# A windowed attention block with its MLP and divisive normalisation, in fp32: the first normalised set is copied by VectorE instead of ScalarE, the MLP's way down is split around the transposes, and odd halves take their fourth strip from the other end

## The chip, the cores and the metric

The kernel runs on one core of a Trainium2 chip. The metric is the device time of one execution in microseconds, the median over several executions. A core has five engines that run their own instruction streams and wait for each other by semaphores: TensorE (PE in the profile, with PEld for its weight loads), VectorE (DVE), ScalarE (ACT), GpSimd (POOL) and SyncE (SP), which here issues the DMAs. TensorE reads SBUF and writes PSUM; PSUM has eight banks, all of them in use.

## What is computed

The input is (4, 96, 128, 128) in fp32: four images of 96 channels. The block does layer normalisation over the channels, attention with 6 heads of 16 in shifted windows of 8x8 tokens, a projection and a residual, a second layer normalisation, an MLP of 96 to 384 to 96 with an exact GELU and a second residual, and at last a generalised divisive normalisation over the channels. Cut to what matters:

```python
y = _ln(x, norm1_w, norm1_b)
y = jnp.roll(y, (-ss, -ss), axis=(1, 2))
y = y.reshape(B, H // ws, ws, W // ws, ws, C).transpose(0, 1, 3, 2, 4, 5).reshape(-1, N, C)
qkv = y @ qkv_w.T + qkv_b
...
attn = jnp.einsum('bhnd,bhmd->bhnm', q, k) + mask
attn = jax.nn.softmax(attn, axis=-1)
out = jnp.einsum('bhnm,bhmd->bnhd', attn, v).reshape(-1, N, C) @ proj_w.T + proj_b
...
x = shortcut + out
h1 = jax.nn.gelu(_ln(x, norm2_w, norm2_b) @ mlp_w1.T + mlp_b1, approximate=False)
x = x + (h1 @ mlp_w2.T + mlp_b2)
...
denom_sq = jnp.einsum('nchw,ic->nihw', x * x, gamma_eff) + beta_eff
return x * jax.lax.rsqrt(denom_sq)
```

The mask is not zero only for windows in the last row and in the last column of windows of an image.

## The kernel before

The image is cut into 64 units of 8 rows (16 windows of 64 tokens), and a unit into two halves of 8 windows (512 tokens). There are 128 halves, numbered A; an even half holds windows 0 to 7 of its unit and an odd half windows 8 to 15. The kernel is a software pipeline, written out by hand: in round H each engine runs its list of stages (a function `steps` for each engine), each stage on the half H + offset. The offsets are TURN_IN 4 (transposes of the input to tokens by channels, and statistics), TURN_OUT 3 (normalised tokens transposed back), QK 1, ATTEND 0, PROJECT -2, MLP -3, UP -4 (up to 384), SETTLE -5 (down to 96), DIVIDE -6. So a round holds one stage each of several halves, and the time is about 128 rounds. Order between engines comes from semaphores alone.

The stages that matter here, in the order in which a round takes them:

- TensorE: `scores` (k and q of six windows per strip; windows' masks are added by one more small matmul each, line 1045), `project_k` and `project_q`, `times_v` (line 1061), `denominators`, `sum_probs`, `project`, `mlp_down` (lines 1108 and 1111), `turn_run` (transposes of the probabilities, line 936, mixed with those of both normalised sets, line 942), `project_v` (line 1007), `mlp_up` 0 and 1 (line 1096), `turn_in` of the input and of the second residual stream (lines 923 and 928), `mlp_up` 2.
- VectorE: row maxima and subtraction of the scores (`max_scores`, `shift_scores`, lines 792 and 799, first for the fourth strip in `pv_bank`, then for three banks), `normalise` twice, `first_residual` (815), `divide` (808), `second_residual` (824), `outputs` (830), `split_y2` (770: the low part of the second normalised set), `v_blocks` (783, four copies), `statistics` (721, eight), `variances` (734 to 743).
- ScalarE: copies of k and q (556, 550), four exponentials (564), logarithms and inverses, an activation table load (514), `y2_copy` (544: the high part of the second normalised set), `y1_copy` (538: the first normalised set, two instructions of 96x256, out of PSUM into window order), copies of the transposed probabilities (575), three GELUs (593), a table load.

The channels of a half lie in strips: with 96 channels in groups of 32, three groups fill partitions 0 to 95, and partitions 96 to 127 hold a fourth strip, which takes a fourth part of the half's tokens. In the attention, `in_strips` puts three pairs of windows (MAIN, 384 tokens) in the three groups and the pair LAST in the fourth strip; `divide` writes `attended`, and `move_attended` carries the fourth strip by three DMAs to its place.

Two waits tie the first normalised set to other stages. `split_y2` has `dve.wait_ge(y_ready[0], ...)` beside its own `y_ready[1]`, and `turn_in` waits for `y_ready[0]` and `y2_split`, since it writes to the banks (`turn_banks`) that hold both sets. `y_ready[0]` is raised by `y1_copy`, `y_ready[1]` by `y2_copy`. The banks of `mlp_up` are handed on in a fixed order (`MM_ITEMS`): `mlp_up` 0 waits for `x2_ready` (`first_residual`), `mlp_up` 1 for `x3_ready` (`second_residual`), `mlp_up` 2 for the first GELU.

Of the kernel before, what the change touches and what calls it, by code (L numbers as in the profile page):

```python
# [23 lines left out]
HEADS, WIN, SHIFT = 6, 8, 4  # L24
# [43 lines left out]
def window_block(nc, x, qmask, kmask, ident, head_mask, ones_pair, norm1_w, norm1_b, qkv_t, qkv_b,  # L68
# [8 lines left out]
    with ctx:  # L77
# [229 lines left out]

        SOFTMAX_ORDER = (GROUPS, 0, 1, 2)
# [14 lines left out]
        def _(sp):  # L323
# [46 lines left out]
            def move_attended(A):  # L370

                wait_alone(sp, attended_ready, A + 1)
                for j in range(HEAD_PAIRS):
                    sp.dma_start(attended[group(j), MAIN:HALF], attended[strip, group(j, 128)])\
                        .then_inc(attended_moved, 16)
# [127 lines left out]
        def _(act):  # L503
# [27 lines left out]
            def y1_copy(A):  # L531
                act.wait_ge(y_turned[0], 2 * (A + 1))
                by_window = y1[0:DIM, unit_slot(A, Y_SLOTS), :]\
                    .rearrange("c (n q x) -> c n q x", q=WIN, x=WIN)[:, :, chunks_of(A)[0]:chunks_of(A)[-1] + 1, :]
                for r in range(2):
                    dst = by_window[:, r * HALF_WINDOWS:(r + 1) * HALF_WINDOWS, :, :]
                    src = normed_columns(0)[:, :, r, :].rearrange("c q (n x) -> c n q x", x=WIN)
                    made = nc.scalar.activation(dst, src, ACT.Copy)  # L538
                made.then_inc(y_ready[0], 1)

# [18 lines left out]
            def softmax_exp(A, g):  # L559
# [3 lines left out]
                dst = probs[:, :, LAST, :, :] if g == GROUPS else probs[:, g, 0:LAST, :, :]  # L563
# [45 lines left out]
            def steps(run, H):  # L609
# [15 lines left out]
                run(y1_copy, TURN_OUT)  # L625
# [11 lines left out]
        def _(dve):  # L637
# [126 lines left out]
            def split_y2(A):  # L764

                dve.wait_ge(y_ready[1], A + 1)
                dve.wait_ge(y_ready[0], min(A - MLP + TURN_OUT + 1, HALVES))
                lo, hi = (half_of(tile[0:DIM, :], A).rearrange("c (q r t) -> c q r t", r=2, t=64)
                          for tile in (y2_lo, y2_hi))
                nc.vector.tensor_tensor(lo, normed_columns(1), hi, ALU.subtract).then_inc(y2_split, 1)  # L770

# [32 lines left out]
            def divide(A):  # L804
# [3 lines left out]
                nc.vector.tensor_tensor(attended[:, 0:MAIN], pv_bank[:, 0:MAIN], inv_sum[:, :],  # L808
# [25 lines left out]
            def steps(run, H):  # L834
# [31 lines left out]
        def _(pe):  # L866
# [118 lines left out]

            def project_k(A):
# [6 lines left out]
                in_strips(mm_bank("k", A), wk, y1_windows(A, 0, 2 * LAST), y1_windows(A, 2 * LAST))\  # L993
                    .then_inc(k_made, 1)

            def project_q(A):
# [3 lines left out]
                in_strips(mm_bank("q", A), wq, y1_windows(A, 0, 2 * LAST), y1_windows(A, 2 * LAST))\  # L1000
# [49 lines left out]
            def times_v(A):  # L1050
# [5 lines left out]
                for turn in range(2 * LAST):  # L1056
                    at, n = turn // 2, turn % 2
                    first = turn * TOKENS
                    for s in range(STRIPS):
                        m, p = (s, at) if s < HEAD_PAIRS else (at, LAST)  # L1060
# [6 lines left out]
            def sum_probs(A):  # L1067
# [3 lines left out]
                for m in range(HEAD_PAIRS):  # L1071
                    nc.tensor.matmul(sum_bank[group(m), 0:MAIN], ones_pair_sb[:, :],
                                     probs_t[:, A % 2, m, 0:LAST, :], start=True, stop=True)
                for m in range(HEAD_PAIRS):
                    made = nc.tensor.matmul(sum_bank[strip, group(m, 128)], ones_pair_sb[:, :],  # L1075
                                            probs_t[:, A % 2, m, LAST, :], start=True, stop=True)
# [23 lines left out]
            def mlp_down(A):  # L1100

                pe.wait_ge(gelu_ready, HID_CHUNKS * (A + 1))
                mm_wait("mlp2", A)
                to = mm_bank("mlp2", A)
                for n in range(HID_CHUNKS):
# [7 lines left out]
                made.then_inc(mlp2_made, 1)  # L1113
# [6 lines left out]
            def steps(run, H):  # L1120
# [20 lines left out]
                run(turn_in, PROJECT, 1)  # L1141
                run(mlp_up, UP, 2)
# [54 lines left out]
```

## Time and profile before

| | |
|---|---|
| median of 3 runs | 1757.68 us (1756.24 to 1758.75) |
| profiled execution, its own time | 1756.11 us |
| span of the profiled execution | 1754.3 us |
| mean granted TensorE clock | 0.991 |
| busy: PE, PEld, DVE, ACT, POOL | 95%, 83%, 81%, 85%, 21% |

The span is the time from the first to the last instruction of the core; the execution's own time is 1.8 us more. A busy share is an average over the whole span, and PE's counts matmuls whose ends are modelled.

### The profile page before, as it was taken

What the parts mean: (1) busy time and instruction counts of PE and PEld (TensorE: products, weight loads), DVE (VectorE), ACT (ScalarE), POOL (GpSimd) and SP (SyncE); (2) the same over time, 40 slices, a digit from 0 to 9 for tenths busy, and PEclk for the clock granted to TensorE, in tenths of its full rate; (3) what the DMA queues carried; (4) which work ended last, traced back from release to release, by engine and by line L of the source; (5) the groups of instructions that cost most, each with busy time, mean ns of one, the idle gap of its engine ahead of it and who ended that gap; (6) DMA issues with size and microseconds to landing.
All of it is one profiled execution on the core that took longest, in us unless ns stands there. A gap on an engine that the chain in (4) does not pass through costs nothing.

```text
span 1754.3 us, 83088 instructions
## 1 busy us (share of the span) xinstructions
PE 1662.1 (95%) x33524; PEld 1464.1 (83%) x33524; DVE 1423.0 (81%) x4142; ACT 1487.8 (85%) x2957; POOL 361.1 (21%) x459
## 2 busy tenths in 40 slices
PE   5899999999999999999999999999999999999995
PEld 3688888888888888888888888888888888888874
DVE  5788888888888888888888888888888888888871
ACT  2688888888888888888888888888888888888884
POOL 2121221221221221221221221221222222222111
PEclk9999999999999999999999999999999999999997
DMA  2112122122122122122122122122121222222111
GB/s 57 47 51 64 55 61 62 54 64 59 55 61 62 54 61 62 54 67 57 54 69 56 53 68 57 53 68 57 55 66 56 56 66 57 57 64 57 46 34 32
DMA packets 179169, 100.38 MB, mean 57 GB/s; under 512 B 26868, under 2 KB 178790, under 8 KB 178790
## 3 DMA queue, kind: packets, MB, share of 16 engines
q1 hardware_dynamic: 178228, 94.96, 19.5%
q8 instruction: 269, 4.41, 1.1%
q14 instruction: 110, 0.90, 0.2%
q10 hardware_dynamic: 562, 0.11, 0.0%
HBM read 32.05 MB, written 25.17 MB: 33 GB/s over the span
## 4 chain that ended last, share of the span: by engine, by line
PE 71%; DVE 17%; issue 5%; ACT 5%; DMA 1%; SPq 0%; POOL 0%; DVEq 0%; POOLq 0%
PE mm_bank L906 10%; PE mm_bank L1111 10%; PE mm_bank L1096 8%; PE score_banks L936 7%; PE pv_bank L1061 6%; PE mm_bank L904 6%; DVE stats L721 5%; PE mm_bank L1108 5%; PE pv_bank L1007 4%; DVE v_block L783 4%; PE turn_banks L942 4%; PE score_banks L1075 3%; PE score_banks L1037 3%; DVE row_max L792 2%; DVE shifted L799 2%
## 5 line engine op out<-in xcount | busy, mean ns | idle before, releaser
L514 ACT ACT_TABLE_LOAD x256 | 328.4, 1283 | 4.6
L564 ACT ACTIVATE probs<-shifted 128x384 f32<-128x384 f32 x512 | 265.7, 519 | 32.0 <-DVE shifted L799 29.0
L1108 PE MATMUL mm_bank<-hidden,w 128*32 128x384 f32 x2304 | 277.4, 492 | 0.1
L1111 PE MATMUL mm_bank<-hidden,w 128*32 128x128 f32 x2304 | 276.8, 275 | 0.0
L593 ACT ACTIVATE hidden<-mm_bank 128x512 f32<-128x512 f32 x384 | 238.4, 621 | 42.2 <-PE mm_bank L1096 41.5
L1111 PEld LDWEIGHTS mm_bank<-hidden,w 128*32 128x32 f32 x2304 | 254.4, 111 | 1.2
L469 POOL TENSOR_TENSOR x<-x,b_bias 128x384 f32<-128x384 f32 x128 | 105.7, 826 | 716.7 <-PE turn_banks L928 716.7
L770 DVE TENSOR_TENSOR y_lo<-turn_banks,y_hi 96x512 fp32r<-96x512 f32 x128 | 87.9, 687 | 197.2 <-ACT y L538 194.3
L575 ACT ACTIVATE probs_t<-score_banks 128x512 f32<-128x512 f32 x384 | 220.1, 617 | 0.0
L792 DVE TENSOR_REDUCE row_max<-score_banks 128x6 f32<-128x384 f32 x384 | 199.4, 547 | 0.0
L799 DVE TENSOR_TENSOR shifted<-score_banks,row_max 128x384 f32<-128x384 f32 x384 | 199.3, 546 | 0.0
L721 DVE BATCH_NORM_STATS2 stats<-turn_banks 128x6 f32<-128x96 f32 x1024 | 181.7, 249 | 17.1 <-PE turn_banks L923 11.2
L783 DVE COPY v_block<-pv_bank 64x192 f32<-64x192 f32 x512 | 180.4, 352 | 11.7 <-PE pv_bank L1007 6.5
L936 PE MATMUL score_banks<-ident_sb,probs 64*128 64x64 f32 x3072 | 181.8, 229 | 4.0 <-ACT probs L564 2.3
L1096 PE MATMUL mm_bank<-y_hi,w_hi 97*128 97x512 f32 x384 | 172.9, 450 | 0.1
L936 PEld LDWEIGHTS score_banks<-ident_sb,probs 64*128 64x128 f32 x3072 | 146.5, 138 | 30.0 <-issue 24.4
L1061 PEld LDWEIGHTS pv_bank<-probs_t,v_block 128*32 128x32 f32 x6144 | 97.2, 110 | 74.6 <-issue 74.1
L1061 PE MATMUL pv_bank<-probs_t,v_block 128*32 128x64 f32 x6144 | 114.3, 221 | 44.4 <-DVE shifted L799 40.5
L1096 PE MATMUL mm_bank<-y_lo,w_hi 97*128 97x512 f32 x384 | 152.0, 396 | 0.0
L1096 PE MATMUL mm_bank<-y_hi,w_lo 97*128 97x512 f32 x384 | 150.6, 392 | 0.0
L1037 PE MATMUL pv_bank<-k_block,q 32*64 32x128 f32 x1536 | 147.5, 284 | 0.0
L1007 PE MATMUL pv_bank<-wv,y 97*128 97x96 f32 x1024 | 145.8, 286 | 0.0
(110 smaller groups left out, 4568.1 us busy)
## 6 DMA issues: line engine op xcount, KB each, us to landing
x_ext<-in_x SPq DMA_DIRECT2D x128, 192.0 KB, 3.2
k_block<-k SPq DMA_DIRECT2D x256, 96.0 KB, 2.0
out<-o_ext SPq DMA_DIRECT2D x64, 192.0 KB, 2.8
x_ext<-in_x SPq DMA_DIRECT2D x128, 48.0 KB, 2.8
attended<-attended SPq DMA_DIRECT2D x384, 16.0 KB, 1.8
x<-x SPq DMA_DIRECT2D x384, 16.0 KB, 1.8
out<-o_ext SPq DMA_DIRECT2D x64, 96.0 KB, 2.6
out<-o_ext SPq DMA_DIRECT2D x128, 48.0 KB, 2.1
```

Source lines behind the costliest of these rows:

```text
L514: nc.scalar.preload_act_table_set(name)
L564: nc.scalar.activation(dst, shifted[:, g, :, :].rearrange("t (i e) k -> t i e k", e=TILE_HEADS), ACT.Exp).then_inc(probs_ready, 1)
L593: nc.scalar.activation(hidden[:, n, :], mm_bank(f"mlp1_{n}", A)[:, :], ACT.Gelu)\
L721: made = nc.vector.bn_stats(stats[:, (H + 1) % 2, ln, n, :], chunk)
L783: made = nc.vector.tensor_copy(to, values[:, :, :, e, :])
L792: nc.vector.tensor_reduce(row_max[:, g, :], group_scores(g), op=ALU.max, axis=AX.X)\
L799: nc.vector.tensor_tensor(shifted[:, g, :, :], group_scores(g), row_max[:, g, :].unsqueeze(2) .broadcast_to([128, LAST * TILE_HEADS, TOKENS]),
L936: return nc.tensor.transpose(score_banks[:, bank, first:first + TOKENS], probs[half, m, p, :, :], ident_sb[half, half])
L1061: made = nc.tensor.matmul(pv_bank[group(s), first:first + TOKENS], v_block[:, (A % 2) * HALF_WINDOWS + 2 * p + n, m, :], probs_t[:, A % 2, ...
L1096: made = nc.tensor.matmul(mm_bank(f"mlp1_{n}", A)[:, :], w[:, cols], tokens, start=part == 0, stop=part == 2)
L1108: nc.tensor.matmul(to[group(j), 0:MAIN], w2[:, n, group(j)], hidden[:, n, 128:HALF], start=first, stop=last)
L1111: made = nc.tensor.matmul(to[strip, group(n, 128)], w2[:, c, group(n)], hidden[:, c, 0:128], start=c == 0, stop=c == HID_CHUNKS - 1)
```

## The change

It has three parts.

1. `y1_copy` goes from ScalarE to VectorE, as two copies of 96x256 that come behind `split_y2` and ahead of `v_blocks`. `split_y2` no longer waits for `y_ready[0]`. On VectorE, `outputs` now comes ahead of `second_residual`.
2. `mlp_down` gets the list of its steps: steps 0 and 1 are done ahead of `turn_run` and step 2 behind it. `mlp_up` 1 goes behind both `turn_in`.
3. In odd halves the main pairs of windows are 1 to 3 and the fourth strip takes pair 0, where it took pair 3. In even halves nothing changes. The same number of instructions works on the same sizes; window 15, the only masked one of most odd halves, now lies in the main strips.

```diff
+        def main_pairs(A):
+            return range(A % 2, A % 2 + LAST)
+        def side_pair(A):
+            return 0 if A % 2 else LAST
+        def main_tokens(A):
+            return slice(A % 2 * 128, A % 2 * 128 + MAIN)
+        def side_tokens(A):
+            return slice(side_pair(A) * 128, side_pair(A) * 128 + 128)
...
                 for j in range(HEAD_PAIRS):
-                    sp.dma_start(attended[group(j), MAIN:HALF], attended[strip, group(j, 128)])\
+                    first = main_tokens(A).start + 128 * j
+                    sp.dma_start(attended[group(j), side_tokens(A)], attended[strip, first:first + 128])\
                         .then_inc(attended_moved, 16)
...
-            def y1_copy(A):
-                act.wait_ge(y_turned[0], 2 * (A + 1))
...
-                    made = nc.scalar.activation(dst, src, ACT.Copy)
-                made.then_inc(y_ready[0], 1)
...
                 run(y2_copy, MLP)
-                run(y1_copy, TURN_OUT)
                 run(probs_t_copy, ATTEND, 0)
...
             def split_y2(A):
                 dve.wait_ge(y_ready[1], A + 1)
-                dve.wait_ge(y_ready[0], min(A - MLP + TURN_OUT + 1, HALVES))
...
+            def y1_copy(A):
+                dve.wait_ge(y_turned[0], 2 * (A + 1))
...
+                for r in range(2):
+                    dst = by_window[:, r * HALF_WINDOWS:(r + 1) * HALF_WINDOWS, :, :]
+                    src = normed_columns(0)[:, :, r, :].rearrange("c q (n x) -> c n q x", x=WIN)
+                    made = nc.vector.tensor_copy(dst, src)
+                made.then_inc(y_ready[0], 1)
...
                 run(divide, ATTEND - 1)
+                run(outputs, DIVIDE)
                 run(second_residual, SETTLE)
-                run(outputs, DIVIDE)
                 run(split_y2, MLP)
+                run(y1_copy, TURN_OUT)
                 run(v_blocks, ATTEND)
...
             def window_of(A, r, i, n):
-                return (A % 2) * HALF_WINDOWS + 2 * (LAST if r == GROUPS else i) + n
+                return (A % 2) * HALF_WINDOWS + 2 * (side_pair(A) if r == GROUPS else main_pairs(A)[i]) + n
...
-            def mlp_down(A):
-                pe.wait_ge(gelu_ready, HID_CHUNKS * (A + 1))
-                mm_wait("mlp2", A)
+            def mlp_down(A, steps):
+                if steps[0] == 0:
+                    pe.wait_ge(gelu_ready, HID_CHUNKS * (A + 1))
+                    mm_wait("mlp2", A)
...
-                for n in range(HID_CHUNKS):
+                for n in steps:
...
-                made.then_inc(mlp2_made, 1)
+                if steps[-1] == HID_CHUNKS - 1:
+                    made.then_inc(mlp2_made, 1)
...
-                run(mlp_down, SETTLE)
+                run(mlp_down, SETTLE, range(0, 2))
                 turn_run(H)
+                run(mlp_down, SETTLE, range(2, HID_CHUNKS))
                 run(project_v, ATTEND)
                 run(mlp_up, UP, 0)
-                run(mlp_up, UP, 1)
                 run(turn_in, TURN_IN, 0)
...
                 run(turn_in, PROJECT, 1)
+                run(mlp_up, UP, 1)
                 run(mlp_up, UP, 2)
```

The first place is VectorE in the middle of a round, from `first_residual` on. The row of before, with the semaphores that each instruction waits for (`y_ready1` is `y1_copy`'s, `y_ready2` is `y2_copy`'s):

```order
L815 TENSOR_TENSOR x<-mm_bank,x_ext 128x384 [waits x3_ready,x_biased,proj_made]
L808 TENSOR_TENSOR attended<-pv_bank,inv_sum 128x384 [waits proj_made,pv_made,inv_sum_ready]
L824 TENSOR_TENSOR x<-mm_bank,x 128x384 [waits out_ready,sq_ready,x2_biased,mlp2_made]
L830 TENSOR_TENSOR o_ext<-x,inv_den 128x6x64 [waits out_stored1,inv_den_ready]
L770 TENSOR_TENSOR y_lo<-turn_banks,y_hi 96x512 [waits y_ready1,y_ready2]
L783 COPY v_block<-pv_bank 64x4x3x16 [waits v_made]
L783 COPY v_block<-pv_bank 64x4x3x16 x3
```

And the same place with the change:

```order
L831 TENSOR_TENSOR x<-mm_bank,x_ext 128x384 [waits x3_ready,x_biased,proj_made]
L824 TENSOR_TENSOR attended<-pv_bank,inv_sum 128x384 [waits proj_made,pv_made,inv_sum_ready]
L846 TENSOR_TENSOR o_ext<-x,inv_den 128x6x64 [waits out_stored1,inv_den_ready]
L840 TENSOR_TENSOR x<-mm_bank,x 128x384 [waits out_ready,sq_ready,x2_biased,mlp2_made]
L776 TENSOR_TENSOR y_lo<-turn_banks,y_hi 96x512 [waits y_ready2]
L785 COPY y<-turn_banks 96x8x32 [waits y_turned1]
L785 COPY y<-turn_banks 96x8x32
L799 COPY v_block<-pv_bank 64x4x3x16 [waits v_made]
L799 COPY v_block<-pv_bank 64x4x3x16 x3
```

`second_residual` now stands directly ahead of `split_y2`, and the two copies of the first normalised set stand between `split_y2` and the four copies of v.

The second place is TensorE from the last transpose of `turn_run` to the end of `mlp_up`. Before:

```order
L936 MATMUL score_banks<-ident_sb,probs 128x64
L1007 MATMUL pv_bank<-wv,y1 128x96 x4
L1096 MATMUL mm_bank0<-y2_hi,w1_hi 128x512
L1096 MATMUL mm_bank0<-y2_hi,w1_lo 128x512
L1096 MATMUL mm_bank0<-y2_lo,w1_hi 128x512
L1096 MATMUL mm_bank1<-y2_hi,w1_hi 128x512
L1096 MATMUL mm_bank1<-y2_hi,w1_lo 128x512
L1096 MATMUL mm_bank1<-y2_lo,w1_hi 128x512
L923 MATMUL turn_banks<-ident_sb,x_ext 128x96 x4
L928 MATMUL turn_banks<-ident_sb,x2 128x128 x3
```

With the change:

```order
L953 MATMUL score_banks<-ident_sb,probs 128x64
L1131 MATMUL mm_bank1<-hidden,w2 32x384 x3
L1134 MATMUL mm_bank1<-hidden,w2 32x128 x3
L1029 MATMUL pv_bank<-wv,y1 128x96 x4
L1118 MATMUL mm_bank0<-y2_hi,w1_hi 128x512
L1118 MATMUL mm_bank0<-y2_hi,w1_lo 128x512
L1118 MATMUL mm_bank0<-y2_lo,w1_hi 128x512
L940 MATMUL turn_banks<-ident_sb,x_ext 128x96 x4
L945 MATMUL turn_banks<-ident_sb,x2 128x128 x3
L1118 MATMUL mm_bank1<-y2_hi,w1_hi 128x512
```

The last step of the way down now follows the transposes, and only one of the two `mlp_up` groups is left between `project_v` and `turn_in`.

The third place is TensorE in `scores` of an odd half with one masked window. Before:

```order
L1037 MATMUL score_banks<-k_block,q 64x128 x6
L1037 MATMUL pv_bank<-k_block,q 64x128 x2
L1045 MATMUL pv_bank<-k_masks,q_quadrants 64x128
L1037 MATMUL score_banks<-k_block,q 64x128 x6
L1037 MATMUL pv_bank<-k_block,q 64x128 x2
L1045 MATMUL pv_bank<-k_masks,q_quadrants 64x128
L1037 MATMUL score_banks<-k_block,q 64x128 x6
L1037 MATMUL pv_bank<-k_block,q 64x128 x2
L1045 MATMUL pv_bank<-k_masks,q_quadrants 64x128
L904 MATMUL mm_bank1<-y1,wk 32x384 x3
```

With the change:

```order
L1059 MATMUL score_banks<-k_block,q 64x128 x6
L1059 MATMUL pv_bank<-k_block,q 64x128 x2
L1059 MATMUL score_banks<-k_block,q 64x128 x6
L1059 MATMUL pv_bank<-k_block,q 64x128 x2
L1059 MATMUL score_banks<-k_block,q 64x128 x6
L1059 MATMUL pv_bank<-k_block,q 64x128 x2
L1067 MATMUL score_banks<-k_masks,q_quadrants 64x128 x3
L921 MATMUL mm_bank1<-y1,wk 32x384 x3
```

The three mask matmuls went from one group of partitions, one behind each set of scores, to three different groups of partitions, all behind the last set.

## Rows read from the trace of the kernel before

**Rows 1.** The page: busy time, share and instructions of each engine.

```profile
PE 1662.1 (95%) x33524; PEld 1464.1 (83%) x33524; DVE 1423.0 (81%) x4142; ACT 1487.8 (85%) x2957; POOL 361.1 (21%) x459
```

**Rows 2.** Waits from 100 to 1700 us: total, times, longest.

```profile
DVE y_lo L770 <- ACT y L538: 189.0, 119, 1.6
...
PE pv_bank L1061 <- DVE shifted L799: 39.9, 60, 1.3
```

**Rows 3.** Timeline of VectorE, 806 to 812 us: start, length, what.

```profile
806.20 0.69 DVE L770 TENSOR_TENSOR y_lo<-turn_banks,y_hi 96x512 fp32r<-96x512 f32 x1 [1.58 <-ACT y L538]
806.80 1.45 DVE L783 COPY v_block<-pv_bank 64x192 f32<-64x192 f32 x4
808.28 1.42 DVE L721 BATCH_NORM_STATS2 stats<-turn_banks 128x6 f32<-128x96 f32 x8
...
811.12 0.56 DVE L799 TENSOR_TENSOR shifted<-pv_bank,row_max 128x384 f32<-128x384 f32 x1
```

**Rows 4.** Timeline of TensorE, 811 to 821 us.

```profile
811.83 0.88 PE L1061 MATMUL pv_bank<-probs_t,v_block 128*32 128x64 f32 x48 [0.67 <-DVE shifted L799]
...
814.45 0.52 PE L1108 MATMUL mm_bank<-hidden,w 128*32 128x384 f32 x3
...
816.06 0.52 PE L1108 MATMUL mm_bank<-hidden,w 128*32 128x384 f32 x3
...
816.58 0.77 PE L936 MATMUL score_banks<-ident_sb,probs 64*128 64x64 f32 x17
...
817.83 0.22 PE L936 MATMUL score_banks<-ident_sb,probs 64*128 64x64 f32 x1
817.99 1.13 PE L1007 MATMUL pv_bank<-wv,y 97*128 97x96 f32 x8
818.90 0.47 PE L1096 MATMUL mm_bank<-y_hi,w_hi 97*128 97x512 f32 x1
...
820.36 0.49 PE L923 MATMUL turn_banks<-ident_sb,x_ext 96*128 96x96 f32 x4
```

**Rows 5.** Timeline of VectorE, 815 to 820 us.

```profile
815.07 0.45 DVE L760 TENSOR_TENSOR y_tok<-turn_banks,rstd 128x288 f32<-128x288 f32 x1
815.44 0.55 DVE L815 TENSOR_TENSOR x<-mm_bank,x_ext 128x384 f32<-128x384 f32 x1
...
816.68 0.56 DVE L824 TENSOR_TENSOR x<-mm_bank,x 128x384 f32<-128x384 f32 x1 [0.23 <-PE mm_bank L1111]
817.16 0.55 DVE L830 TENSOR_TENSOR o_ext<-x,inv_den 128x384 f32<-128x384 f32 x1
...
819.30 0.69 DVE L770 TENSOR_TENSOR y_lo<-turn_banks,y_hi 96x512 fp32r<-96x512 f32 x1 [1.59 <-ACT y L538]
```

**Rows 6.** Timeline of ScalarE, 816 to 819 us.

```profile
816.19 1.28 ACT L514 ACT_TABLE_LOAD   x1
818.06 0.59 ACT L544 ACTIVATE y_hi<-turn_banks 96x512 fp32r<-96x512 f32 x1 [0.58 <-PE turn_banks L942]
```

**Rows 7.** Timeline of TensorE: scores, k, q and the next product with v.

```profile
808.72 0.35 PE L1037 MATMUL score_banks<-k_block,q 32*64 32x128 f32 x6
...
809.63 0.52 PE L904 MATMUL mm_bank<-y,wk 97*32 97x384 f32 x3
...
821.82 0.35 PE L1037 MATMUL score_banks<-k_block,q 32*64 32x128 f32 x6
...
823.32 0.52 PE L904 MATMUL mm_bank<-y,wk 97*32 97x384 f32 x3
...
824.31 0.50 PE L904 MATMUL mm_bank<-y,wq 97*32 97x384 f32 x3
...
824.91 0.88 PE L1061 MATMUL pv_bank<-probs_t,v_block 128*32 128x64 f32 x48
```

**Rows 8.** Groups of VectorE instructions by shape: count, busy us, mean ns, idle before.

```profile
L783 DVE COPY v_block<-pv_bank 64x192 f32<-64x192 f32 x512 | 180.4, 352 | 11.7 <-PE pv_bank L1007 6.5
...
L701 DVE CAST w_hi<-w 97x384 fp32r<-97x384 f32 x1 | 0.4, 352 | 0.0
```

More of the change, by code:

```diff
@@ L529, in rstd_pair @@
                     .then_inc(rstd_ready, 1)
-            def y1_copy(A):
-                act.wait_ge(y_turned[0], 2 * (A + 1))
[L533 to L537, printed above, removed]
-                    made = nc.scalar.activation(dst, src, ACT.Copy)
-                made.then_inc(y_ready[0], 1)
             def y2_copy(A):
@@ L562, in softmax_exp @@
                     wait(act, probs_turned[bank], A)
-                dst = probs[:, :, LAST, :, :] if g == GROUPS else probs[:, g, 0:LAST, :, :]
+                pairs = slice(main_pairs(A)[0], main_pairs(A)[-1] + 1)
+                dst = probs[:, :, side_pair(A), :, :] if g == GROUPS else probs[:, g, pairs, :, :]
                 nc.scalar.activation(dst, shifted[:, g, :, :].rearrange("t (i e) k -> t i e k", e=TILE_HEADS),
@@ L770, in split_y2 @@
                 nc.vector.tensor_tensor(lo, normed_columns(1), hi, ALU.subtract).then_inc(y2_split, 1)
+            def y1_copy(A):
+                dve.wait_ge(y_turned[0], 2 * (A + 1))
+                by_window = y1[0:DIM, unit_slot(A, Y_SLOTS), :]\
+                    .rearrange("c (n q x) -> c n q x", q=WIN, x=WIN)[:, :, chunks_of(A)[0]:chunks_of(A)[-1] + 1, :]
+                for r in range(2):
[3 more added lines that the diff above has]
+                made.then_inc(y_ready[0], 1)
             def v_blocks(A):
@@ L807, in divide @@
                 wait(dve, proj_made, A)
-                nc.vector.tensor_tensor(attended[:, 0:MAIN], pv_bank[:, 0:MAIN], inv_sum[:, :],
+                nc.vector.tensor_tensor(attended[:, main_tokens(A)], pv_bank[:, 0:MAIN], inv_sum[:, :],
                                         ALU.mult).then_inc(attended_ready, 1)
@@ L984, in turn_run, with qk_windows @@
                             made.then_inc(probs_turned[2], 1)
+            def qk_windows(A):
+                side = 2 * side_pair(A)
+                return y1_windows(A, 2 * main_pairs(A)[0], 2 * main_pairs(A)[-1] + 2), y1_windows(A, side, side + 2)
             def project_k(A):
@@ L992, in project_k @@
                 mm_wait("k", A)
-                in_strips(mm_bank("k", A), wk, y1_windows(A, 0, 2 * LAST), y1_windows(A, 2 * LAST))\
+                in_strips(mm_bank("k", A), wk, *qk_windows(A))\
                     .then_inc(k_made, 1)
@@ L999, in project_q @@
                 mm_wait("q", A)
-                in_strips(mm_bank("q", A), wq, y1_windows(A, 0, 2 * LAST), y1_windows(A, 2 * LAST))\
+                in_strips(mm_bank("q", A), wq, *qk_windows(A))\
                     .then_inc(q_made, 1)
@@ L1059, in times_v @@
                     for s in range(STRIPS):
-                        m, p = (s, at) if s < HEAD_PAIRS else (at, LAST)
+                        m, p = (s, main_pairs(A)[at]) if s < HEAD_PAIRS else (at, side_pair(A))
                         made = nc.tensor.matmul(pv_bank[group(s), first:first + TOKENS],
@@ L1072, in sum_probs @@
                     nc.tensor.matmul(sum_bank[group(m), 0:MAIN], ones_pair_sb[:, :],
-                                     probs_t[:, A % 2, m, 0:LAST, :], start=True, stop=True)
+                                     probs_t[:, A % 2, m, main_pairs(A)[0]:main_pairs(A)[-1] + 1, :], start=True, stop=True)
                 for m in range(HEAD_PAIRS):
                     made = nc.tensor.matmul(sum_bank[strip, group(m, 128)], ones_pair_sb[:, :],
-                                            probs_t[:, A % 2, m, LAST, :], start=True, stop=True)
+                                            probs_t[:, A % 2, m, side_pair(A), :], start=True, stop=True)
                 made.then_inc(sums_made, 1)
```

## The prediction

> **What bounds the kernel now.** The page alone points at TensorE: 95% busy, ScalarE 85%, VectorE 81% [rows 1]. But ends of matmuls are modelled, so I read the waits next. Two matter [rows 2]: VectorE's `split_y2` waits for ScalarE's `y1_copy` in 119 rounds, 1.6 us each, and TensorE's product with v (line 1061) waits for the subtraction of the fourth strip's maxima (799) in 60 rounds, 0.67 us each. So TensorE does wait, in every other round. Then the timeline. I count from the start of `times_v` in one round, 811.83 = 0, and write places as such offsets.
>
> VectorE's side [rows 3]: once `split_y2` starts, it works without a stop: the four copies of v start 0.60 later, statistics and variances follow, the strip's subtraction ends at 811.68, and `times_v` starts at 811.83. From `split_y2` to `times_v` are 5.63, from the copies of v to it 5.03. TensorE's side [rows 4]: from `times_v` to the way down 2.62, the way down in six blocks of (816.06 - 814.45) / 5 = 0.32, the transposes at 4.75, the next work behind them (`project_v`) at 6.16. Then ScalarE: y2 at 6.23 [rows 6], y1 behind it, and `split_y2` at 819.30 - 811.83 = 7.47 [rows 5]. 7.47 + 5.61 = 13.08 (it ends at 824.91 [rows 7]), the round; from one `split_y2` to the next it is 13.10 [rows 3, 5]. This loop goes through all three engines: TensorE to the last transpose, ScalarE for two copies, VectorE to the subtraction. It holds in odd rounds too. There TensorE's scores take 823.32 - 821.82 = 1.50 where the even round's take 0.91 [rows 7], because of the masked window. But q's last block starts at 824.31, TensorE would be free at 824.63, and `times_v` starts at 824.91, when VectorE is done. TensorE has about 0.3 to spare in odd rounds and 0.85 in even ones. So the 0.59 for the masks is hidden today.
>
> **The change, part by part.**
>
> *Way down split.* Four of six blocks stay ahead of the transposes: they start 2 x 0.32 = 0.65 earlier, at 4.10, and end, with the 1.41 from 816.58 to 817.99 [rows 4], at 5.51. What they need is there: `normalise` ends at 815.07 + 0.45 = 815.52 [rows 5], offset 3.69, and ScalarE's last exponential stands two instructions of the same size ahead of the table load at 816.19 [rows 6], so it ends near 815.3. ScalarE's table load ends at 816.19 + 1.28 = 817.47, offset 5.64 [rows 6]; y2's copy then runs 5.64 to 6.23, and `split_y2` could start at 6.34, with the 0.11 from copy to VectorE. That is 1.1 earlier than today.
>
> *But `second_residual` is late now.* It waits for the whole way down. The two blocks behind the transposes start at 5.51 and 5.83; today VectorE starts 816.68 - 816.06 = 0.62 behind the last block's start [rows 4, 5], so 6.45. It stands ahead of `split_y2` and holds it for 0.48, the distance to the next instruction (816.68 to 817.16 [rows 5]). So `split_y2` starts at 6.93, not 6.34: it gains 0.54, where the waits of [rows 2] seemed to promise 1.6. `outputs` ahead of it costs nothing; it falls into VectorE's idle time between 4.5 and 6.45.
>
> *Two copies on VectorE.* They lie on the chain. No row shows a 96x256 copy on VectorE. A 128x384 instruction takes 0.55 and a 128x288 one 0.45, 1.04 ns an element; 256 elements give 0.42 busy [rows 5]. What counts is the distance from start to start: 0.60 for 512 elements [rows 3], 0.37 for 288 (815.07 to 815.44 [rows 5]), so 0.34 for 256. Two are 0.68. The other bound is the copies of v: four of 192 elements take (808.28 - 806.80) / 4 = 0.37 each, more than their busy 0.352 [rows 3, 8]; with 64 elements more (0.067) that is 0.43, two are 0.86. I take 0.68, since the copies of v alternate between partitions 0 and 64, and y1's all stand at partition 0, as the instructions of [rows 5] do.
>
> The Trainium skill (VectorE: DVE Perf Modes, section "Two Vector instructions with no wait between them") says it as a rule: an instruction waits for all earlier ones when its start quadrant differs from that of the last access, else it may start into the tail of the one before. By this rule the trace agrees: 0.37 against 0.352 busy for v, 0.46 to 0.48 against 0.55 for the rest. By the rule the pair costs 0.68, without it 0.86.
>
> *Sum.* v's copies start at 6.93 + 0.60 + 0.68 = 8.21, today at 8.07. The round is 8.21 + 5.03 = 13.24 against 13.10: 0.14 longer. Over 128 rounds that is 18 us. Fill and drain lack some stages, and I leave them as they are.
>
> *TensorE's path, to see that it doesn't bind.* `turn_in` waits for y1's second copy: 6.93 + 0.60 + 0.34 + 0.42 = 8.29, plus 0.15 from VectorE to TensorE (811.68 to 811.83 [rows 3, 4]) is 8.44. Today `turn_in` starts at 8.53 [rows 4] and scores follow 1.46 later [rows 4, 7]. Now a second `mlp_up` lies between, which I take at 0.70 (two fill 818.90 to 820.36, 0.73 each with the first one's start-up [rows 4]): scores at 10.60. Even rounds: 0.91 for them, 1.33 for k and q, `times_v` possible at 12.84, below 13.24. Odd rounds with today's masks: 13.43, above it. So the fourth strip's move matters: its three masks go to three groups of partitions, where tiles work beside each other: the even round's 0.91 holds three sets of eight tiles, 0.04 a tile, so three masks cost some 0.11: 12.95. It saves TensorE 0.48 in 64 rounds and the kernel nothing against today, because VectorE ends last. TensorE idles near 0.65 ahead of `turn_in`; today's stall of 0.67 [rows 4] in every other round goes with a mean granted clock of 0.991, so I cost no fall to 1.2 GHz.
>
> *The others.* ScalarE loses two copies, and its GELU for `mlp_up` 2 comes some 0.6 later, with the table load and the copies of k and q behind it; in today's odd rounds all of that comes 0.59 later too, behind the longer scores [rows 7], and the loop doesn't notice. x3's three DMAs on SP's queue start 1.6 later (`second_residual` at 6.45, today 4.85), behind them those of `attended`; `square` and the product that read x3 come much later, behind `turn_in`'s `bias_x2` on POOL. I cost both at nothing; were x3 late, `denominators` at 0.66 of the next round would wait, one for one.
>
> **Rivals.**
>
> *Copies at full distance.* 0.86 instead of 0.68 puts 0.17 more into each round: 13.41, or 0.31 x 128 = 40 us, 1797. For it: v's copies, the only PSUM copies in the trace. Against: their alternating partitions.
>
> *The masks stay in line.* If they cost 0.59 in main strips too, TensorE binds odd rounds at 13.43: 0.19 x 64 = 12 us more, 1788. It decides from 0.4 us upward. Against it: they lie on three groups of partitions, as the tiles of a set do.
>
> *No pause behind the transposes.* TensorE pauses between shapes: 0.20 before the transposes and 0.16 behind them (817.83 to 817.99 [rows 4]). If the way down's second part starts without the 0.16, VectorE gains it: 0.14 - 0.16, no change, 1756. Against: the shapes still change there. The split also adds one such change, ahead of `project_v`, 0.16 to 0.20 by these rows; it falls into the 0.65 ahead of `turn_in` and costs nothing (without that cover, 0.16 x 128 = 20 us). The Trainium skill (TensorEngine Tiling (Array Packing), "Key Properties") says that changing the tiling mode drains TensorE. By this rule, with which the two pauses agree, the 0.16 stays and my sum holds; without the rule the round would be today's.
>
> *Faster: copies at double rate.* Line 701 converts 384 elements in 352 ns [rows 8], where 384 take 0.55 [rows 5], so a one-source instruction can run at two elements a cycle. Then 256 elements cost 0.20 from start to start, two 0.40: 0.14 - 0.28 = -0.14, 18 us less, 1740. It decides below 0.27 a copy. Against: line 701 reads SBUF; v's copies read PSUM, as y1's do, and their 352 ns for 192 elements is the slow rate.
>
> **How the numbers follow.** The sum 0.14 x 128 = 18 us is made against the profiled execution's 1756.11 us, 1.6 below the median, so 1774 there and 1776 as a median. Chances: my sum 0.5; full distance 0.13; masks in line or another path of TensorE 0.12; no change 0.13; double rate, or a gain that I don't see, 0.12. All but the last two are slower: 0.75. A measurement of this kernel tells about 0.2% (3.5 us) from nothing. The range 1754 to 1798 leaves out only the faster cases and holds the others; if only slower ones are counted, it is 1766 to 1798.
>
> **What would show it.** Between `split_y2` starts 13.2 to 13.3 us in odd and even rounds; `split_y2` waiting for `second_residual` and not for ScalarE; y1's copies 0.42 busy and 0.34 apart; an idle TensorE of 0.5 to 0.8 ahead of line 940 in nearly every round, and one of 0.3 ahead of line 1083 that waits for line 815; masks behind the scores in about 0.1. I am wrong if the round is under 13.1, which needs a shorter distance from the transposes to v's copies than 2.70, or if TensorE arrives last in `times_v`.

## The result and the profile after

The change makes the kernel 1.1% slower. Its median is 1777.85 us (1773.97 to 1778.8, 4 runs), against 1756.96 us (1756.02 to 1758.75, 4 runs) for the kernel before: a ratio of 1.0113, 95% interval 1.0098 to 1.0127. The forecast was 1776.

The profiled execution took 1773.97 us, with a span of 1772.2 and a granted clock of 0.993. The page, where [rows 1] had 95, 83, 81, 85 and 21%:

```profile
span 1772.2 us, 82960 instructions
PE 1676.4 (95%) x33524; PEld 1422.3 (80%) x33524; DVE 1494.0 (84%) x4398; ACT 1436.4 (81%) x2701; POOL 366.1 (21%) x459
```

VectorE's busy time has grown by 71 us and ScalarE's has shrunk by 51. Then the waits of the same stretch as [rows 2], 100 to 1700 us: engine, line and what it waited for, us in total, times, longest.

```profile
ACT hidden L601 <- PE mm_bank L1118: 196.7, 240, 1.3
DVE x L840 <- PE mm_bank L1134: 166.5, 121, 1.7
PEld turn_banks L940 <- issue: 73.9, 118, 0.6
...
POOL x_sq L493 <- DMA x<-x: 36.3, 33, 2.0
...
PE pv_bank L1083 <- DVE shifted L815: 15.4, 53, 1.0
```

`split_y2`'s wait of 1.6 us for ScalarE is gone. In its place, in 121 rounds, VectorE waits 1.4 for the end of the way down, in `second_residual` (840). The timeline shows the piece of VectorE that answers to [rows 3, 5]: start, duration, instruction, and the idle time ahead of it in brackets.

```profile
824.17 0.56 DVE L840 TENSOR_TENSOR x<-mm_bank,x 128x384 f32<-128x384 f32 x1 [1.46 <-PE mm_bank L1134]
824.65 0.68 DVE L776 TENSOR_TENSOR y_lo<-turn_banks,y_hi 96x512 fp32r<-96x512 f32 x1
825.25 0.74 DVE L785 COPY y<-turn_banks 96x256 f32<-96x256 f32 x2
825.91 1.45 DVE L799 COPY v_block<-pv_bank 64x192 f32<-64x192 f32 x4
827.39 1.42 DVE L728 BATCH_NORM_STATS2 stats<-turn_banks 128x6 f32<-128x96 f32 x8
828.91 0.29 DVE L741 TENSOR_TENSOR mean_gap<-stats 128x8 f32<-128x8 f32 x1
829.12 0.16 DVE L743 TENSOR_TENSOR within<-stats 128x8 f32<-128x8 f32 x1
```

And TensorE, for [rows 4]. `times_v` (1083) of this round had started at 817.63.

```profile
823.22 0.52 PE L1131 MATMUL mm_bank<-hidden,w 128*32 128x384 f32 x3
...
823.57 0.50 PE L1131 MATMUL mm_bank<-hidden,w 128*32 128x384 f32 x3
...
824.01 1.13 PE L1029 MATMUL pv_bank<-wv,y 97*128 97x96 f32 x8
...
826.09 0.52 PE L940 MATMUL turn_banks<-ident_sb,x_ext 96*128 96x96 f32 x4 [0.23 <-issue]
...
828.99 0.45 PE L1067 MATMUL score_banks<-k_masks,q_quadrants 4*64 4x128 f32 x6
...
830.89 0.49 PE L1083 MATMUL pv_bank<-probs_t,v_block 128*32 128x64 f32 x21
```

The second part of the way down starts at 823.22 - 817.63 = 5.59 behind `times_v`, and `second_residual` at 6.54. This round is 0.1 late in all of it: the medians over 110 rounds are 5.49 and 6.45, where 5.51 and 6.45 had been worked out. Places given from here on as one number are such medians, counted from the start of `times_v`.

From one `times_v` to the next I took the distance over 110 rounds of each timeline, from the tenth on. The median was 13.088 and is 13.175; 99 of the 110 rounds lay within 0.02 of it, and now 59 do. The mean was 13.106 and is 13.225: 0.119 x 128 = 15 of the 18 us between the two spans. Of these, 0.087 x 128 = 11 us are in the regular round, and 4 come from single longer rounds: 7 of 110 were over 13.2, up to 13.6, and 25 are, up to 14.15. The rest is in the first and last rounds. So the total is as forecast, but the forecast had 0.14 in every round.

One instruction leads further. `mean_gap` is a subtraction of 128x8 elements, and VectorE's other instructions of its size take 0.16 or 0.17. It took 0.29 here, and in other rounds 0.17, or up to 0.7 (once 0.99). In the same trace, this is where it is alone:

```profile
1371.79 0.17 DVE L741 TENSOR_TENSOR mean_gap<-stats 128x8 f32<-128x8 f32 x1
```

And this is a slow round, GpSimd's `square` (line 493) and VectorE's `mean_gap`:

```profile
1596.09 1.04 POOL L493 TENSOR_TENSOR x_sq<-x 96x512 f32<-96x512 f32 x1 [0.49 <-DMA x<-x]
...
1596.57 0.59 DVE L741 TENSOR_TENSOR mean_gap<-stats 128x8 f32<-128x8 f32 x1
```

`square` ends at 1596.09 + 1.04 = 1597.13 and `mean_gap` at 1596.57 + 0.59 = 1597.16: they end together. In the round above `mean_gap` ends at 829.20, and `square`:

```profile
828.13 1.03 POOL L493 TENSOR_TENSOR x_sq<-x 96x512 f32<-96x512 f32 x1 [0.19 <-issue]
```

It ends at 829.16. In the whole stretch `mean_gap` takes over 0.2 in 101 of 121 rounds, and in all 101 it ends 0.02 to 0.03 behind a `square`. The 119 `mean_gap` of 128x8 took 332 ns each before, and take 296 with the change. So the kernel before already paid some 0.15 here, in nearly every round, inside the 5.03 us that the prediction took over as VectorE's work. Its lines, from the round that ends at 824.91:

```profile
822.15 1.03 POOL L476 TENSOR_TENSOR x_sq<-x 96x512 f32<-96x512 f32 x1
822.90 0.31 DVE L734 TENSOR_TENSOR mean_gap<-stats 128x8 f32<-128x8 f32 x1
```

From `square`'s start to the next `times_v` are 824.91 - 822.15 = 2.76, and with the change 830.89 - 828.13 = 2.76 too. The medians say the same: `square` started at 10.33 and starts at 10.42, and 2.76 later the round is over, at 13.09 and at 13.175. So in both kernels it is `square` that sets the end of the regular round. Before, it started as soon as GpSimd's `bias_x2` was done; now it starts 0.26 behind the landing of x3's DMAs (1.76 before).

### The profile page after: what moved, and what is told of

It reads as the page before. It is cut to its first block, busy times and chain, and to the rows that moved or that the text cites. A ratio compares the mean times of both kernels' runs of the same rounds, so it can differ in the third digit from the quotient of the medians.

```text
span 1772.2 us, 82960 instructions
## 1 busy us (share of the span) xinstructions
PE 1676.4 (95%) x33524; PEld 1422.3 (80%) x33524; DVE 1494.0 (84%) x4398; ACT 1436.4 (81%) x2701; POOL 366.1 (21%) x459
## 4 chain that ended last, share of the span: by engine, by line
PE 73%; DVE 20%; issue 4%; DMA 1%; ACT 1%; SPq 0%; POOL 0%; DVEq 0%; POOLq 0%; ACTq 0%
PE mm_bank L923 10%; PE mm_bank L1134 10%; PE mm_bank L1118 8%; PE score_banks L953 7%; PE pv_bank L1083 6%; PE mm_bank L1131 6%; PE mm_bank L921 6%; DVE stats L728 5%; PE pv_bank L1029 4%; PE turn_banks L959 4%; PE score_banks L1059 3%; DVE v_block L799 3%; PE score_banks L1097 3%; DVE y L785 2%; PE turn_banks L940 2%
## 5 line engine op out<-in xcount | busy, mean ns | idle before, releaser
L601 ACT ACTIVATE hidden<-mm_bank 128x512 f32<-128x512 f32 x384 | 229.3, 597 | 221.7 <-PE mm_bank L1118 209.8
L1131 PE MATMUL mm_bank<-hidden,w 128*32 128x384 f32 x2304 | 302.3, 495 | 0.1
L1134 PE MATMUL mm_bank<-hidden,w 128*32 128x128 f32 x2304 | 300.5, 276 | 0.0
L1134 PEld LDWEIGHTS mm_bank<-hidden,w 128*32 128x32 f32 x2304 | 243.6, 111 | 1.2
L840 DVE TENSOR_TENSOR x<-mm_bank,x 128x384 f32<-128x384 f32 x128 | 71.4, 558 | 178.5 <-PE mm_bank L1134 178.5
L583 ACT ACTIVATE probs_t<-score_banks 128x512 f32<-128x512 f32 x384 | 212.7, 591 | 0.9 <-PE score_banks L953 0.8
L728 DVE BATCH_NORM_STATS2 stats<-turn_banks 128x6 f32<-128x96 f32 x1024 | 182.0, 251 | 12.4 <-PE turn_banks L940 7.0
L493 POOL TENSOR_TENSOR x_sq<-x 96x512 f32<-96x512 f32 x128 | 132.7, 1037 | 78.2 <-DMA x<-x 61.6
L1029 PEld LDWEIGHTS pv_bank<-wv,y 97*128 97x128 f32 x1024 | 124.7, 192 | 24.8 <-issue 24.4
```

The costliest lines, as they stand in the source:

```text
L583: nc.scalar.activation(dst, src, ACT.Copy).then_inc(probs_t_ready, 1)
L601: nc.scalar.activation(hidden[:, n, :], mm_bank(f"mlp1_{n}", A)[:, :], ACT.Gelu)\
L728: made = nc.vector.bn_stats(stats[:, (H + 1) % 2, ln, n, :], chunk)
L1029: made = nc.tensor.matmul(pv_bank[:, p * DIM:(p + 1) * DIM], y1_windows(A, 2 * p, 2 * p + 2), wv[:, :], start=True, stop=True)
L1131: nc.tensor.matmul(to[group(j), 0:MAIN], w2[:, n, group(j)], hidden[:, n, 128:HALF], start=first, stop=last)
L1134: made = nc.tensor.matmul(to[strip, group(n, 128)], w2[:, c, group(n)], hidden[:, c, 0:128], start=c == 0, stop=c == HID_CHUNKS - 1)
```

## The experiments

All times are medians. The kernel before, run again beside them, has 1757.4 us beside e3, e4, e5 and e7, 1757.2 beside e6, e8, e9 and e10, and 1758.2 beside e11 and e12. "Round" is the median distance of `times_v`, in even and in odd rounds where they differ.

| kernel | us | ratio to before, 95% interval | round |
|---|---|---|---|
| before | 1757 | | 13.09 |
| after | 1777.85 | 1.0113 [1.0098, 1.0127] | 13.17 |
| e3_way_whole | 1746.62 | 0.9936 [0.9922, 0.9951] | 12.99 |
| e4_strip_back | 1792.39 | 1.0201 [1.0184, 1.0218] | 13.18 / 13.44 |
| e5_square_late | 1761.56 | 1.0023 [1.0012, 1.0034] | 13.06 |
| e7_copy_back | 1760.71 | 1.0011 [1.0001, 1.0021] | 13.17, 17 of 110 at 12.4 to 12.6 |
| e6_before_square_late | 1741.19 | 0.9900 [0.9876, 0.9924] | 12.94 |
| e8_copy_back_square_late | 1706.74 | 0.9711 [0.9687, 0.9736] | 12.45 / 12.64 |
| e9_strip_back_square_late | 1727.43 | 0.9820 [0.9795, 0.9844] | 12.45 / 13.04 |
| e10_way_whole_square_late | 1741.72 | 0.9903 [0.9882, 0.9924] | 12.94 / 12.97 |
| e11_up_ahead_square_late | 1759.62 | 1.0009 [0.9999, 1.0020] | 13.05 |
| e12_residual_behind_square_late | 1748.32 | 0.9949 [0.9932, 0.9965] | 12.90 |

**e3_way_whole**: the changed kernel with the way down whole again, ahead of the transposes, and `second_residual` ahead of `outputs`.

```diff
+                run(second_residual, SETTLE)
                 run(outputs, DIVIDE)
-                run(second_residual, SETTLE)
...
-                run(mlp_down, SETTLE, range(0, 2))
+                run(mlp_down, SETTLE, range(0, HID_CHUNKS))
                 turn_run(H)
-                run(mlp_down, SETTLE, range(2, HID_CHUNKS))
```

> The changed kernel with the way down whole again, ahead of the transposes, and second_residual ahead of outputs as before; y1's copies stay on VectorE, mlp_up 1 stays behind turn_in. My theory (VectorE's chain ends last): the transposes start at 4.75 after times_v, y2's copy ends near 6.82, split_y2 starts at 6.93, the same as the 6.92 of the changed kernel, so v's copies start at 8.18 again. The split buys nothing. But second_residual comes 1.6 us earlier, x3's DMAs land earlier, and GpSimd's square is over when mean_gap starts: round 13.06 to 13.12, no rounds of 13.4 and more, 1754 to 1762 us. Rival (only the start of split_y2 counts, GpSimd doesn't): as the changed kernel, 1774 to 1779. Rival (TensorE's pauses between shapes and its idle ahead of turn_in set the time): one pause of 0.16 less in each round, and 13.0, 1757.

Measured: 1746.62, below the range and below the kernel before. `split_y2` starts at 6.85, `mean_gap` takes 177 ns on average, and the round is 12.99. With y1 off ScalarE and x3 early, `square` starts at 10.12, and it ends 0.03 behind the start of `mean_gap` (11.12). So the split of the way down, with the order that goes with it on VectorE, costs this kernel 31 us; 16 of them go when `square` is moved (e5).

**e4_strip_back**: the changed kernel with the fourth strip on pair 3 in odd halves too.

```diff
-            return range(A % 2, A % 2 + LAST)
+            return range(0, LAST)
...
-            return 0 if A % 2 else LAST
+            return LAST
...
-            return slice(A % 2 * 128, A % 2 * 128 + MAIN)
+            return slice(0, MAIN)
```

> The changed kernel with the fourth strip taken from pair 3 in odd halves too. My theory: the masks cost 0.59 in odd rounds again instead of 0.11. TensorE reaches times_v at 10.53 + 1.50 + 1.33 = 13.36 or later in odd rounds, where VectorE allows 13.17; even rounds stay. Odd rounds 13.4 to 13.45, 60 of them: 12 to 17 us more than the changed kernel, 1789 to 1794. Rival (the strip's end changes nothing, VectorE ends last in any case): 1777.

Measured: 1792.39, inside the range. Odd rounds are 13.44, where the prediction had 13.43 for TensorE with today's masks. That it fits so well is luck in part: scores start 0.07 earlier than forecast, and k and q take 0.07 more (1.40 from the start of k to `times_v`, where TensorE doesn't wait).

**e5_square_late**: the changed kernel, but `square` on GpSimd also waits for the last step of VectorE's variances (`spread`, the last of the four small ones that begin with `mean_gap`), so the two never run together.

```diff
                 wait_alone(pool, den_made, A)
+                wait_alone(pool, spread_ready, spread_count(min(A - SETTLE, HALVES - 1 - PROJECT)))
```

> The changed kernel with one more wait: GpSimd's square waits for spread_ready of its round, so it never runs beside mean_gap, the first VectorE instruction with two inputs in SBUF. My theory (mean_gap ends only when GpSimd's square ends): mean_gap takes 0.17 in every round, the round is 13.05 as in the few rounds of the changed kernel where the square came late by itself, and none has 13.4 or more apart from the last rows' masks: 1755 to 1762 us. Rival (the irregular rounds come from the DMAs or from TensorE, and the square's place doesn't matter): 1774 to 1779. Rival (the square ends too late for the denominators): they start later than 0.67 after times_v and the time goes up.

Measured: 1761.56, inside the range. A wait added to GpSimd makes the kernel 16 us faster than the changed one. By form:

```profile
L742 DVE TENSOR_TENSOR mean_gap<-stats 128x8 f32<-128x8 f32 x119 | 20.6, 173 | 12.7 <-DVE stats L729 0.5
```

**e7_copy_back**: the changed kernel with y1's copies back on ScalarE, and `split_y2` waiting for them again.

```diff
                 run(y2_copy, MLP)
+                run(y1_copy, TURN_OUT)
...
                 dve.wait_ge(y_ready[1], A + 1)
+                dve.wait_ge(y_ready[0], min(A - MLP + TURN_OUT + 1, HALVES))
...
                 run(split_y2, MLP)
-                run(y1_copy, TURN_OUT)
```

> The changed kernel with y1's copy back on ScalarE behind y2's, and split_y2 waiting for it again; way down, mlp_up and strip as changed. My theory: the copies on ScalarE end near 6.85, beside second_residual, so split_y2 starts at 6.93 to 7.05 as now, but v's copies follow 0.60 later, at 7.53 to 7.65 and not 8.18. TensorE could do 12.4 and doesn't bind: round 12.5 to 12.7, 60 us less than before: 1690 to 1710. Rival (VectorE's two copies cost little, and the split of the way down with its pause is what slowed the kernel): 1765 to 1780. Rival (ScalarE becomes the bound when its chain has both copies and the later GELUs): 12.9 to 13.1, 1735 to 1757.

Measured: 1760.71, a miss of 50 us. The copies are gone from VectorE, and the round is 13.17 all the same, as in the changed kernel. In 17 rounds of 110 it is 12.4 to 12.6. The timeline of one of the others, GpSimd, SyncE's queue and VectorE:

```profile
828.52 1.83 SPq L398 DMA_DIRECT2D x<-x  x3
...
830.42 0.83 POOL L486 TENSOR_TENSOR x<-x,b_bias 128x384 f32<-128x384 f32 x1 [2.97 <-PE turn_banks L946]
831.86 1.04 POOL L493 TENSOR_TENSOR x_sq<-x 96x512 f32<-96x512 f32 x1 [0.61 <-DMA x<-x]
...
830.43 1.42 DVE L739 BATCH_NORM_STATS2 stats<-turn_banks 128x6 f32<-128x96 f32 x8
831.95 0.97 DVE L752 TENSOR_TENSOR mean_gap<-stats 128x8 f32<-128x8 f32 x1
832.84 0.16 DVE L754 TENSOR_TENSOR within<-stats 128x8 f32<-128x8 f32 x1
```

VectorE is ready at 831.95 and gets no further than `square`, which ends at 832.90 and had waited for x3's DMAs (828.52). Those had waited for `second_residual`. This is a second loop: last transpose, second part of the way down, `second_residual`, x3's DMAs, `square`, `mean_gap`, the strip's maxima, `times_v`. `square` starts at 10.42 here as in the changed kernel, 3.97 behind `second_residual`, and `times_v` comes 2.76 after it: 13.17 to 13.18, whoever copies y1.

**e6_before_square_late**: the same line added to `square` in the kernel before.

> The kernel before, in which GpSimd's square of x3 (x_sq) waits for VectorE's product that follows mean_gap (spread_ready), so that it never runs beside mean_gap. Theory of contention: mean_gap takes 0.17 us instead of 0.31 to 0.33, the strip's maxima come 0.15 earlier and every round ends on VectorE, so the regular round goes from 13.09 to 12.94 us: 0.15 x 128 = 19 us less, 1738 us (1733 to 1745). Rival, the gap's length is not due to GpSimd: mean_gap stays at 0.3, the time within 0.2% of 1757. Second rival, a later square is late for the denominators at the head of the next round: they start after 0.67 and the time goes up, 1760 or more.

Measured: 1741.19, inside the range, round 12.94 as expected. `mean_gap` is at 173 ns, from 332.

**e8_copy_back_square_late**: e7 with the late `square`.

> The changed kernel with y1's copies back on ScalarE (split_y2 waits for them) and the square late as well. Theory: the split of the way down and the shorter masks are worth some 0.5 us a round once the pair of copies is off VectorE and nothing lengthens mean_gap. The rounds of 12.51 that a part of the run without the late square showed become the rule: 0.55 x 128 = 70 us less than before, 1690 us (1680 to 1705). Rival, the 0.94 us of mean_gap were a sign of something else that is late in these rounds (x3's DMAs, VectorE's input for it): the round stays at 13.1 and the time near 1757.

Measured: 1706.74, 1.7 above the range, and the fastest of all: 50 us less than the kernel before. Two rounds of its VectorE:

```profile
1134.86 0.56 DVE L843 TENSOR_TENSOR x<-mm_bank,x 128x384 f32<-128x384 f32 x1 [1.36 <-PE mm_bank L1136]
1135.33 0.68 DVE L789 TENSOR_TENSOR y_lo<-turn_banks,y_hi 96x512 fp32r<-96x512 f32 x1
1135.93 1.45 DVE L802 COPY v_block<-pv_bank 64x192 f32<-64x192 f32 x4
...
1138.93 0.17 DVE L753 TENSOR_TENSOR mean_gap<-stats 128x8 f32<-128x8 f32 x1
...
1147.78 0.68 DVE L789 TENSOR_TENSOR y_lo<-turn_banks,y_hi 96x512 fp32r<-96x512 f32 x1
...
1152.20 0.56 DVE L811 TENSOR_REDUCE row_max<-pv_bank 128x6 f32<-128x384 f32 x1 [0.17 <-PE score_banks L1069]
```

`split_y2` comes after 1147.78 - 1135.33 = 12.45 in this round and 12.64 in the next. In the longer of the two the strip's maxima (811) wait 0.17 for TensorE's masked scores, so TensorE ends last there. In the shorter one it does too, by little: k starts at 11.23 in odd and at 11.04 in even rounds, and `times_v` comes 1.40 later in both, while VectorE alone would allow 7.52 + 4.87 = 12.39 (v's copies, and from them to `times_v` in e5; an estimate). The mean of the two medians, 12.54, is the 0.55 a round that I expected. Most of the 17 us above 1690 are single rounds that are longer, up to 13.8: in 110 rounds they add 14.3 us to the medians, and in the kernel before 2.0. Why they occur stays open; the waits show some late x3:

```profile
POOL x_sq L494 <- DMA x<-x: 29.2, 7, 9.1
PE mm_bank L923 <- POOL x_sq L494: 15.1, 6, 5.1
```

**e9_strip_back_square_late**: e8 with e4's edit.

> As the run with y1's copies on ScalarE and the square late, but the fourth strip is pair 3 in odd halves too, as in the kernel before. Theory: TensorE ends odd rounds. With the strip back the changed kernel had odd rounds of 13.43; turn_in starts at 7.98 instead of 8.37 here, so they are 13.04, while even ones stay at 12.5: 64 x 0.5 = 33 us more than with the strip's move, near 1720 us. Rival, the move of the strip is worth nothing here because VectorE ends odd rounds too: the same time as with it.

Measured: 1727.43, 21 us more than e8, where 33 were expected and a time near 1720. Odd rounds are 13.04, as worked out, even ones 12.45; but e8's odd rounds already are 12.64, and 0.40 x 64 is 26, not 33.

```profile
DVE row_max L811 <- PE pv_bank L1069: 38.6, 65, 1.2
```

In 65 rounds VectorE waits 0.59 for the masked scores.

**e10_way_whole_square_late**: e8 with e3's edit.

> As the run with y1's copies on ScalarE and the square late, but the way down is whole ahead of the transposes and second_residual stands ahead of outputs again. Theory: split_y2 starts at 7.47 again (transposes, table load, two copies on ScalarE), the round is 7.47 + 5.61 less the 0.15 of mean_gap, 12.93: 50 us more than with the split, near 1738 us, and about the time of the kernel before with the late square. Rival, the split of the way down brings nothing and the gain is the masks' and the late square's: the same time as with the split, 1690.

Measured: 1741.72, near the 1738 that were expected, and the time of e6. It is 35 us more than e8, not 50, since e8 itself came out 17 above 1690. So with y1 on ScalarE the split is worth 35 us, and moving strip and `mlp_up` without it is worth nothing.

**e11_up_ahead_square_late**: e5 with `mlp_up` 1 back ahead of `turn_in`.

> The changed kernel with the square late (1761.56 us, rounds of 13.05) and, beside that, the second of the three mlp_up ahead of turn_in again, as in the kernel before. Theory: TensorE isn't the bound of these rounds; it has a gap ahead of turn_in that the second mlp_up fills, scores and k come earlier or at the same place, and VectorE still ends the round: 13.05 again, 1761 us (1757 to 1765). Rival, the place of the second mlp_up behind turn_in costs something (GELU, the table load and ScalarE's copies of k and q come late): then the round gets shorter here, 12.99 as in the kernel with the whole way down, 1754 us or less.

Measured: 1759.62, inside the range; the round stays at 13.05, and the runs of the two kernels overlap (1756.9 to 1764.9 here, 1758.8 to 1766.0 in e5). The place of `mlp_up` 1 costs nothing that can be measured.

**e12_residual_behind_square_late**: e5 with `second_residual` behind the copies.

```diff
-                run(second_residual, SETTLE)
                 run(split_y2, MLP)
                 run(y1_copy, TURN_OUT)
+                run(second_residual, SETTLE)
```

> The changed kernel with the square late, and with second_residual behind split_y2 and y1's copies instead of ahead of them. Theory: second_residual held split_y2 at 6.92; without it split_y2 starts when y2's copy is there, 5.66 + 0.59 + 0.11 = 6.36, y1's copies at 6.96, second_residual at 7.64 and the copies of v at 8.12 instead of 8.18: the work on VectorE stays the same and only 0.06 of idle time goes, the round is 12.99 instead of 13.05, 8 us less, 1754 us (1750 to 1760). Rival, the residual's result is then late for x3's DMAs, square and the denominators: 1762 or more.

Measured: 1748.32, 13 us less than e5, a little below the range. Its VectorE:

```profile
823.30 0.69 DVE L777 TENSOR_TENSOR y_lo<-turn_banks,y_hi 96x512 fp32r<-96x512 f32 x1 [1.20 <-ACT y_hi L552]
823.91 0.74 DVE L786 COPY y<-turn_banks 96x256 f32<-96x256 f32 x2
824.57 0.55 DVE L841 TENSOR_TENSOR x<-mm_bank,x 128x384 f32<-128x384 f32 x1
825.04 1.45 DVE L800 COPY v_block<-pv_bank 64x192 f32<-64x192 f32 x4
```

From `split_y2` to the copies of v are 1.74, with `second_residual` among them; ahead of it they were 0.48 + 0.60 + 0.66 = 1.74 too. `split_y2` waits for ScalarE's y2 and starts at 6.29, not at 6.92 less 0.48 = 6.44: that is the 0.16 by which the round is shorter than e5's.

What wasn't tried: y1 on ScalarE without `split_y2` waiting for it, where the two would read the same two PSUM banks together; and e3 with the late `square`.

## Why the prediction came out right, and where it did not

**The total.** 1776 was forecast and 1777.85 measured: direction and size are right. That they are so close is luck in part. The forecast had 0.14 more in every round, from VectorE's chain; measured are 0.087 in the regular round, 4 us in single longer rounds and 3 us at the ends, and the 0.087 is `square`'s later start, not that chain.

**VectorE's chain: right, with one term mis-sized.** `split_y2` starts at 6.92 (6.93 forecast), held by `second_residual` and not by ScalarE. y1's copies start at 7.52 and 0.33 apart:

```profile
L785 DVE COPY y<-turn_banks 96x256 f32<-96x256 f32 x256 | 94.9, 410 | 4.7 <-PE turn_banks L959 4.7
```

410 ns busy were expected as 0.42, the distance as 0.34. The copies of v start at 8.18 (8.21). The step that failed is "from the copies of v to it 5.03", read as VectorE's work without a stop. It had the 0.15 of `mean_gap` beside `square` in it. With `square` out of the way the round is 13.055 (e5) against 12.937 for the kernel before (e6). So the VectorE loop that the prediction describes has grown by 0.12, where 0.14 was said, and e5 against e6 is 20.4 us, where the sum had 18.

**"I cost both at nothing": wrong.** x3's DMAs come 1.6 later, and now `square` waits for them; it starts 0.09 later than before. The prediction looked for the price at `denominators`. It is at `mean_gap`, on another engine: e5 against the changed kernel puts 16 us on it. It also is why the regular round grew by 0.09 only: before, `square` cost 0.15 in nearly every round; now it costs 0.12 in most rounds, 0.4 in some and nothing in a few. The two errors, a cost that was there before and one that is there now, nearly cancel.

**What the copies cost.** Here the kernels with a late `square` stand together, with e3 beside them:

| | y1 on ScalarE | y1 on VectorE |
|---|---|---|
| way down whole | 1741.7 (e10) | not run; e3, without the late square, 1746.6 |
| way down split | 1706.7 (e8) | 1761.6 (e5) |

With y1 on ScalarE the split is worth 35 us, since `split_y2` comes at 6.92 instead of 7.47, and the pair on VectorE takes 55 back: it stands on the chain at full length, 0.66 a round, of which 0.51 show in the regular round, as TensorE holds e8 at 12.54. Without the split, VectorE waits for y1 on ScalarE (e6, e10), so in e3 the pair only replaces that wait, and the round (12.99) is just 0.05 longer than e6's. The prediction priced this pair rightly, but didn't see that the split's gain would be stopped by `square` even without it (e7).

**TensorE's path: right that it doesn't bind, but with less to spare.** `turn_in` at 8.36 (8.44), scores at 10.53 (10.60). The gap in weight loads ahead of `turn_in` is 73.9 / 118 = 0.63 (0.65). Masks: k starts 0.18 later in odd rounds than in even ones, 0.11 forecast; and k and q take 1.40, not 1.33. So TensorE could start `times_v` at 11.64 + 1.40 = 13.04 in odd rounds, where 12.95 was said: in the changed kernel 0.12 are left there, not 0.29, and in e5, at 13.055, next to nothing. The 53 waits for the strip in the table are 0.29 on average, but they aren't in every round. The strip's move saves 14.5 us here (e4), where 13.43 against 13.24 gave 12, and 21 us in e8.

**The rivals.** Copies at full distance: no, 0.33. Double rate: no, 410 ns. Masks in line: no. No pause behind the transposes: no, the way down's second part starts at 5.49 (5.51 forecast), not at 5.35.

## What to carry to other kernels

Before a stretch of an engine is taken as work without a stop, compare the duration of each small instruction in it with others of its size: one that takes twice as long can be a wait that no table of waits lists, and can hide a second loop. A gain on one loop is worth only the distance to the next: here the split brought `split_y2` 0.55 forward, the pair of copies took 0.66, and the DMAs of the delayed step closed a second loop at 13.17 in any case. And where two engines get in each other's way, a wait added to the one with time to spare can make the kernel faster: one line gave 16 us in each of two kernels (e5, e6) and 54 in a third (e8 against e7).

## What the runs showed of the hardware

I had not expected that a VectorE subtraction with both inputs in SBUF, and 8 elements a partition, doesn't end before a GpSimd product that is under way: 0.17 us alone, 0.27 to 0.33 beside the tail of a 1.04 us `square`, 0.97 where it started 0.09 behind it (e7). The Trainium skill (SBUF — State Buffer, section "SBUF: two separate sides") states it: VectorE and GpSimd share a pair of ports under an exclusive lock, which a VectorE operation with two SBUF inputs takes, and whichever starts first keeps it for the whole instruction. The traces agree: both end within 0.04 us of each other in all three places shown. `within` (line 743) and `spread` (line 750) have two SBUF inputs as well and are short there, since they follow when `square` has ended. In e7 there are also rounds the other way about, where `mean_gap` starts just ahead of `square`:

```profile
845.14 0.17 DVE L752 TENSOR_TENSOR mean_gap<-stats 128x8 f32<-128x8 f32 x1
845.15 1.07 POOL L493 TENSOR_TENSOR x_sq<-x 96x512 f32<-96x512 f32 x1 [0.72 <-DMA x<-x]
845.23 1.02 DVE L754 TENSOR_TENSOR within<-stats 128x8 f32<-128x8 f32 x1
```

`mean_gap` is short, and it is `within`, behind it, that ends with `square`. An instruction with one input in SBUF and one in PSUM isn't held: the strip's subtraction (line 815, line 816 in e5) takes 558 ns in the 112 rounds of e5 in which it lies inside `square`, and 558 in the changed kernel, where it mostly runs alone. That the lock itself is the cause no run shows; e5, e6 and e8 show that the delay goes when the two no longer run together.
